# Attention's value products on four column tiles, with the row sums of later units added up on GpSimd first

## The reference

```python
q = (h @ q_w.T + q_b).reshape(b, s, 16, 32)
k = h @ k_w.T + k_b                     # (b, s, 32)
v = h @ v_w.T + v_b                     # (b, s, 32)
scores = einsum('bqhd,bkd->bhqk', q, k) / 32 ** 0.5   # causal mask
attn = softmax(scores, axis=-1)
out = einsum('bhqk,bkd->bqhd', attn, v).reshape(b, s, 512)
return out @ o_w.T + o_b
```

## Time and profile before

| | |
|---|---|
| time, median of 3 runs | 1993.2 us (1989.5, 1994.91, 1993.2) |
| profiled execution, first to last instruction (span) | 1990.9 us |
| mean granted PE clock | 0.991 |
| busy: PE, PEld | 1929.1 us, 1506.0 us |
| busy: DVE, ACT, POOL | 1379.4 us, 860.8 us, 243.7 us |
| value products (L1946), PE busy | 278.3 us |
| masks (L1083), POOL busy | 144.5 us |
| copies out (L951), ACT busy | 76.5 us |

### The profile page before, as it was taken

The page is one execution under the profiler, slowest core; times in us unless marked ns, Lnnn a source line. Parts: engine busy times, 40 slices in busy tenths (PEclk is TensorE's granted clock), DMA queues, the critical chain, the costliest instruction groups (busy, mean ns, idle before and its releaser), DMA issues.

```text
span 1990.9 us, 31329 instructions
## 1 busy us (share of the span) xinstructions
PE 1929.1 (97%) x10816; PEld 1506.0 (76%) x10816; DVE 1379.4 (69%) x3296; ACT 860.8 (43%) x1615; POOL 243.7 (12%) x589
## 2 busy tenths in 40 slices
PE   6999999999999999999999999999999999999998
PEld 3566666666666556556888889999999999999997
DVE  5687777677768656685466887777676777767755
ACT  3366565555556554474222442333333323333221
POOL 2121113211221112122010010010010100101000
PEclk8899999999999999999999999999999999999999
DMA  7443343434433565646346989779788797787884
GB/s 229 129 111 77 91 126 100 112 86 110 108 108 80 143 175 163 207 154 202 137 138 240 360 322 344 286 295 345 285 297 323 294 350 290 292 328 289 326 309 165
DMA packets 116309, 424.32 MB, mean 213 GB/s; under 512 B 28076, under 2 KB 33452, under 8 KB 101944
## 3 DMA queue, kind: packets, MB, share of 16 engines
q1 hardware_dynamic: 104488, 371.92, 55.7%
q10 hardware_dynamic: 11664, 50.40, 6.7%
HBM read 318.16 MB, written 61.10 MB: 190 GB/s over the span
## 4 chain that ended last, share of the span: by engine, by line
PE 47%; DVE 4%; ACT 2%; DMA 1%; issue 1%; SPq 0%; POOL 0%; DVEq 0%; ACTq 0%
PE banks L1786 22%; PE banks L1877 15%; PE banks L1656 8%; PE banks L1946 1%; DVE ln_stats L1220 1%; PE banks L1752 1%; PE banks L1746 1%; DMA upgate_items_dram<-items_ring 1%; DVE x_normed L1232 0%; DVE y L1345 0%; DMA upgate_raw<-in_w_ug 0%; ACT silu_gate L880 0%; PE banks L1923 0%; ACT y_split L865 0%; ACT L880 0%
## 5 line engine op out<-in xcount | busy, mean ns | idle before, releaser
L1877 PE MATMUL banks<-d_ring,y_split 128*128 128x512 f32 x1536 | 377.4, 392 | 1.9 <-DVE y_split L1365 1.9
L973 ACT ACTIVATE probs<-banks 128x512 f32<-128x512 f32 x576 | 313.0, 602 | 53.6 <-PE banks L1923 51.4
L1877 PEld LDWEIGHTS banks<-d_ring,y_split 128*128 128x128 f32 x1536 | 281.7, 188 | 56.8 <-DVE y_split L1365 2.1
L1786 PE MATMUL banks<-h_t_split,items_ring 128*128 128x256 f32 x2280 | 321.1, 283 | 1.9 <-DVE both L1322 1.9
L1786 PEld LDWEIGHTS banks<-h_t_split,items_ring 128*128 128x128 f32 x2280 | 298.8, 191 | 14.0 <-ACT h_t L791 4.0
L1946 PE MATMUL banks<-probs,v_ones 128*64 128x512 f32 (+3 forms) x1536 | 278.3, 497 | 1.0 <-POOL probs L1083 1.0
L1710 PE MATMUL banks<-k_stack,q_stacks 96*128 96x512 f32 (+3 forms) x768 | 251.5, 371 | 11.3 <-DMA q_stacks<-q_split 3.0
L1923 PE MATMUL banks<-q_stacks,k_stack 98*128 98x512 f32 (+3 forms) x768 | 250.7, 368 | 3.5 <-DMA q_stacks<-neg_max_rows 1.8
L1946 PEld LDWEIGHTS banks<-probs,v_ones 128*64 128x64 f32 x1536 | 118.3, 137 | 159.6 <-issue 132.1
L1786 PE MATMUL banks<-input_sums,items_ring 128*128 128x256 f32 x1710 | 236.2, 283 | 0.0
L1083 POOL TENSOR_SCALAR_AFFINE_SELECT probs<-probs 128x128 f32<-128x128 f32 x512 | 144.5, 306 | 666.2 <-ACT probs L973 666.0
(11 more groups left out here) (179 smaller groups left out, 2281.9 us busy)
## 6 DMA issues: line engine op xcount, KB each, us to landing
items_ring<-upgate_items_dram SPq DMA_DIRECT2D x94, 1792.0 KB, 7.3
d_ring<-down_split_dram SPq DMA_DIRECT2D x128, 512.0 KB, 8.0
q_stacks<-q_split SPq DMA_DIRECT2D x192, 128.0 KB, 2.6
o_group<-o_raw SPq DMA_DIRECT2D x128, 128.0 KB, 2.4
upgate_raw<-in_w_ug SPq DMA_DIRECT2D x32, 512.0 KB, 4.3
upgate_items_dram<-items_ring ACTq DMA_DIRECT2D x8, 1792.0 KB, 7.4
upgate_items_dram<-items_made ACTq DMA_DIRECT2D x8, 1792.0 KB, 6.9
x<-in_x SPq DMA_DIRECT2D x32, 256.0 KB, 3.2
```

Of the source, the lines that this page charges most:

```text
L973: nc.scalar.activation(pr[:, u, :], score_bank[:, at % SLOTS_SCORE, :], ACT.Exp, scale=SCALE).then_inc(exped, 1)
L1786: last = nc.tensor.matmul(item_bank(g, item), weights[:, a, item, k * P:(k + 1) * P], by_key(item_input(blk, item, m))[:, k, :], start=(k ...
L1877: last = nc.tensor.matmul(acc[:, t, :], ys[s][:, a, t * P:(t + 1) * P], dr[g % D_RING][:, m, :], start=(f == 0 and a + m == 0), stop=(f == ...
```

## The change

1. `WEIGHED` now names, for each product, one of four rows of 32 columns. Row r takes the query blocks r and r + 4, so each query block's values add up on one row; the bank holds 512 columns, query blocks r and r + 4 of the values in its first two blocks. The bank's other two blocks hold row sums, made by products with a matrix of ones, for query blocks placed by the table. One bank serves a whole head, and heads take turns. Products have at most 256 columns.
2. `sum_first` and `sum_last` are new on GpSimd: the probabilities of units 3 to 6 (queries 512 to 1023, keys 0 to 511) and of unit 7's product of keys 512 to 639 are added up, and part 1 has one product of ones with that sum for each of four query blocks. Part 1 waits for it.
3. `TRIANGLES`' two blocks of one unit are masked by one instruction.
4. One copy of 128x512 a head, five gathers instead of four; `add_halves` and the addition in `invert_sums` go.
5. `probs` gets 14 slots (units 0 to 2 twice, two for the sums); part 0 now takes units 0 to 5. The first modulation weights are loaded by eight DMAs instead of four, to other places.

```diff
+PAIRS, FIRST_UNITS = 4, 3
+SUMMED_UNITS, SUM_AFTER = (3, 4, 5, 6), 7
+PR_SLOTS = 2 * FIRST_UNITS + (NU - FIRST_UNITS) + 2
+FIRST_PART_UNITS = 6
 WEIGHED = [
-    [(0, 0, 0, 0, 512, 0), (1, 4, 1, 512, 512, 0), (0, 3, 0, 512, 512, 0), (1, 1, 1, 128, 384, 0), (1, 1, 3, 384, 128, 384),
-     (0, 2, 6, 768, 256, 256), (1, 2, 2, 256, 256, 0)],
+    [(0, 0, (0, 4)), (1, 0, (1, 5)), (2, 0, (2, 6)), (3, 0, (3, 7)),
+     (1, 1, (1, 5)), (2, 1, (2, 6)), (3, 1, (3, 7)), (0, 1, (4,)), (0, 2, (4,)),
+     (2, 2, (2, 6)), (3, 2, (3, 7)), (1, "sum", ((0, 2), (6, 6))), (0, "sum", ((0, 3), (6, 7))),
+     (1, 2, (5,)), (2, 6, (6,)), (3, 6, (7,))],
...
+def probs_slot(H, u):
+    return H % 2 * FIRST_UNITS + u if u < FIRST_UNITS else FIRST_UNITS + u
@@ SP, gather
-                for half in range(2):
-                    sp.dma_start(og[j * HD:(j + 1) * HD, 2 * half, :], oraw[2 * half * HD:(2 * half + 1) * HD, H % 2, :]).then_inc(gathered[H % 2], 16)
+                for pair in range(PAIRS):
+                    at = (PAIRS - 1 - pair) * 2 * P
+                    sp.dma_start(og[j * HD:(j + 1) * HD, G % 2, at:at + 2 * P], oraw[pair * HD:(pair + 1) * HD, H % 2, 0:2 * P]).then_inc(gathered[H % 2], 16)
@@ ACT, step
-                    if H:
-                        act.wait_ge(pv_done, (H - 1) * PARTS_OF_HEAD + (1 if u <= PART_ENDS[0] else 2))
-                    nc.scalar.activation(pr[:, u, :], score_bank[:, at % SLOTS_SCORE, :], ACT.Exp, scale=SCALE).then_inc(exped, 1)
+                    if H and u >= FIRST_UNITS:
+                        act.wait_ge(pv_done, (H - 1) * PARTS_OF_HEAD + (1 if u < FIRST_PART_UNITS else 2))
+                        act.wait_ge(summed, 3 * (H - 1) + 1)
+                    elif H >= 2:
+                        act.wait_ge(pv_done, (H - 1) * PARTS_OF_HEAD)
+                    nc.scalar.activation(pr[:, probs_slot(H, u), :], score_bank[:, at % SLOTS_SCORE, :], ACT.Exp, scale=SCALE).then_inc(exped, 1)
@@ POOL
+            def sum_first(H):
+                pool.wait_ge(exped, H * NU + SUMMED_UNITS[-1] + 1)
+                if H:
+                    pool.wait_ge(pv_done, H * PARTS_OF_HEAD)
+                first, second = (pr[:, probs_slot(H, u):probs_slot(H, u) + 2, :] for u in SUMMED_UNITS[::2])
+                nc.gpsimd.tensor_tensor(pr[:, PR_SLOTS - 2:PR_SLOTS, :], first, second, ALU.add).then_inc(summed, 1)
+                pool.wait_ge(summed, 3 * H + 1)
+                nc.gpsimd.tensor_tensor(pr[:, PR_SLOTS - 2, :], pr[:, PR_SLOTS - 2, :], pr[:, PR_SLOTS - 1, :], ALU.add).then_inc(summed, 1)
+            def sum_last(H):
+                pool.wait_ge(summed, 3 * H + 2)
+                pool.wait_ge(masked, H * len(TRIANGLES) + list(TRIANGLES).index(SUM_AFTER) + 1)
+                nc.gpsimd.tensor_tensor(pr[:, PR_SLOTS - 2, :], pr[:, PR_SLOTS - 2, :], pr[:, probs_slot(H, SUM_AFTER), :], ALU.add).then_inc(summed, 1)
...
                 for u in TRIANGLES:
+                    if u == SUM_AFTER:
+                        sum_first(H)
                     if tiles and u == BIAS_UNIT:
                         add_bias(b - 1, tiles[1])
...
+                sum_last(H)
@@ PE, weigh
                 if part == 0:
-                    pe.wait_ge(masked, H * len(TRIANGLES) + 3)
-                    pe.wait_ge(exped, H * NU + PART_ENDS[0] + 1)
+                    pe.wait_ge(masked, H * len(TRIANGLES) + FIRST_UNITS)
+                    pe.wait_ge(exped, H * NU + FIRST_PART_UNITS)
...
                 else:
                     pe.wait_ge(masked, (H + 1) * len(TRIANGLES))
+                    pe.wait_ge(summed, 3 * (H + 1))
+                for i, (row, kt, of) in enumerate(WEIGHED[part]):
+                    if kt == "sum":
+                        places, first, weights = [block(H, key, qt) for key, qt in of], 2, ones[:]
+                    else:
+                        places, first, weights = [block(H, kt, qt) for qt in of], of[0] // PAIRS, vs[:, b % 2, kt, :]
+                    moving = pr_blocks(places[0], places[-1] - places[0], len(places))
+                    out = obank[row * HD:(row + 1) * HD, H % 2, first * P:(first + len(places)) * P]
+                    last = nc.tensor.matmul(out.rearrange("p (a n) -> p a n", n=P), weights, moving, start=row not in begun, stop=part == 1 and last_of[row] == i)
```

More of the change, by code:

```diff
@@ L1162, in invert_sums @@
                 for parity in range(2):
[L1163 to L1173 removed]
+                    dve.wait_ge(gathered[parity], 160 * (G + 1))
+                nc.vector.reciprocal(sums[:], sums[:]).then_inc(sums_inverted, 1)
             def scale_group(G, half):
@@ L1441, in network @@
                     invert_sums(ALL // 4 - 1)
-                if g == 1:
-                    for half in range(2):
-                        add_halves(ALL // 4 - 1, half)
                 if nb < PLAIN and f in HAD_STEPS:
@@ L1501, in step @@
                         projection_weights(2 * PROJECTION_STEPS.index(H) + k)
-                side_step(begin[:1])
-                if begin and H > 4:
-                    for half in range(2):
-                        add_halves(G, half)
-                side_step(begin[1:])
+                side_step(begin)
                 for u in range(NU):
@@ L1870, in down @@
                             side_drained(pe, r)
-                        for c in range(2):
-                            pe.wait_ge(o_copied[c], ALL)
+                        pe.wait_ge(o_copied, ALL)
                     elif f == 0:
@@ L1925, in score, with block @@
                 last.then_inc(scored, 1)
+            def block(H, kt, qt):
+                if kt == "all":
+                    return (PR_SLOTS - 2) * HALF + (qt - PAIRS) * P
+                u, col = BLOCKS_AT[kt, qt]
+                return probs_slot(H, u) * HALF + col
             def weigh(H, part):
```

125 lines of the change are left out of this document (56 added, 69 removed), and 3 rows, old and new, of the table WEIGHED.

## The result

The changed kernel takes 2000.29 us (median of 5 runs, 1999.27 to 2001.91) beside 1993.2: ratio 1.0041, 95% interval 1.0030 to 1.0052, slower by about 7 us. 2001 was forecast. The number is right, but most of the way to it is not: two terms of more than ten microseconds each were wrong, with opposite signs. The profiled execution took 1999.27 us with a span of 1997.5.

The account below looks back on a forecast made before the run. TensorE bound the attention by averages, with VectorE level in each head's first half; TensorE's savings and delays from GpSimd's additions summed over head classes to +8.0 us: 1998.9, or 2001.2 beside the median, range 1968 to 2038.

Parts of the forecast that it names:

- -0.62 a head: TensorE's part 0 loses three blocks, 0.66 us, taken as 0.62; over 64 heads -39.7 us if nothing else ends later.
- Rival (c): Parts 0 and 1: issue of weight loads with products binds; 2077 us, half way 2035; chance 0.14 in part or whole.
- The 0.02 for tiles that lose against each other: TensorE: chance 0.02 that four tiles with short products lose against two, 0.9 us a head, 2059 us.
- GpSimd's chain: Three additions and masks each head, the third addition ending at e+6.13; e is the end of unit 6's exponential.
- The step with the most weight: VectorE instructions with two SBUF inputs, and the small negation, wait during GpSimd additions; L1135 ends at e+4.13, was e+2.66.
- rival (a): The negation slips between additions or is not wholly held, so only GpSimd's own chain counts: about 1975 us; chance 0.22.
- the 12.7 us of the plain heads: Plain heads get longer: nine with statistics by +1.13 each, +10.2 us; five without by +0.49 each, +2.5 us.
- The forecast's own sign: L1135's successor: median near 1.4 us confirms, 0.17 means rival (a); head 34's period under 9.4 or over 11.5 refutes.
- With rows: Nine heads with input rows: copy and subtraction behind the negation are held with it; +0.9 us each, +8.1 in all.
- four with 0.4 to 0.7 us more TensorE work before part 1: 0: Heads 5, 6, 13 and 29, without statistics: they add nothing to the span.
- -0.6 each: Nine heads with output tiles, nine with folds: TensorE's extra work covers the 6.2 us of sums; -10.8 us in all.
- The last three heads: Head 63's part 1 waits 6.2 us instead of 3.1, +3.1; heads 61 and 62 meet VectorE's crossing additions, +2.4 together.

Follow-up runs that it names:

- The doubled negation: The changed kernel with the 128x8 negation of the maxima done twice in a row: 2029.51 us, ratio 1.0182 to the kernel before.
- the sums left out: The changed kernel without GpSimd's three additions a head and all waits for them, output differs: 1957.3 us, ratio 0.9825 to the kernel before.
- The filled waits: The kernel with the late wait, plus nine unread products in each step behind heads 13, 29 and 45, where TensorE was idle: 1984.55 us, ratio 0.9959.
- the late wait: The changed kernel with part 1's wait for the sums moved ahead of its last four products: 1993.32 us, ratio 1.0006 to the kernel before.

## Why the prediction was right, and where it was not

**TensorE: right.** -0.62 a head was forecast, -0.65 came, all of it in part 0. Four tiles of 32 columns run side by side: 7 blocks at 0.22 us are 1.54 of the 1.65 us. Rival (c), the limit by issue, falls: part 0 has 32 loads with their products in 1.65 us, 52 ns each, part 1 40 in 1.86, 46 ns, below the 62 ns from which the rival decides. (The prediction's "42 ns a pair" for its own plan is 49, 3.52 us over 72 pairs.) The 0.02 for tiles that lose against each other falls with it.

**GpSimd's chain: size right, 0.4 us too long.** The 128x1024 addition has a median of 2.38 us (2.45 taken), the masks together 0.65 (0.81), so the third ends at e+5.7, not e+6.13.

**The step with the most weight failed in place, not in kind.** "L1135 needs its result, meets the second addition and ends at e+4.13": in the plain heads it slips in 0.02 us ahead of it. That is the mechanism of rival (a), and it took the 12.7 us of the plain heads to 0.2. The forecast's own sign says so: the median of L1187 is 0.168 us, not near 1.4; and head 34's period is 9.40, where under 9.4 was to mean that it is wrong. I had let the held negation end 0.17 us behind the first addition (e+2.68) and the second addition start right there. But a held negation ends with the addition, as the earlier trace rows has it (511.75 and 511.72) and as it is here (504.13 and 504.10), and the second addition starts only 0.08 us behind the first, for whose semaphore it waits (504.10 to 504.18). The doubled negation shows that the hold itself is real: 1.13 us instead of 0.17, 8.3 us in the plain heads and 29 in the total. The gap of 0.08 us stood in no row of before, and (a) had 0.22 where it deserved about as much as the forecast. Its time, 1975, failed as well, by the heads that come next. With rows the same: the negation slips, but the cast behind it is held for 1.51 us, +0.36 a head instead of +0.9.

**The step "four with 0.4 to 0.7 us more TensorE work before part 1: 0" was wrong by 10.8 us**, and "-0.6 each" for heads 45 and 59 by another 8. I looked at what held part 1 there and not at which VectorE instructions read SBUF while GpSimd adds: the keys' cast and subtraction; in head 5 the negation's second half (1.14 us) and the first of the gains' products (1.35 us, 0.44 before); in head 59 a layer norm row of the feed-forward part (1.83 us, 0.76 with the sums left out) and the negation (0.84). The folds of head 59, which read a PSUM bank, keep their 0.74 us. Here are the two rows of head 5:

```profile
132.33 1.14 DVE L1187 SCALAR_TENSOR_TENSOR neg_max<-max_all,neg_max 128x8 fp32r<-128x8 f32 x1 [0.22 <-DVE neg_max L1186]
...
134.23 1.35 DVE L1631 TENSOR_SCALAR x_and_residual<-gain_parts 36x512 f32<-36x512 f32 x1
```

The prediction put the hold to the negation and, in heads with rows, to the copy and subtraction behind it, and should have put it to every such instruction beside the additions. The Trainium skill (SBUF — State Buffer, Who interferes with whom) says that whoever of the two issues first gets the shared ports for its whole instruction ("Issue order, not op shape, decides who blocks"), and it counts casts, where their operands allow it, among the instructions that use the shared ports. The trace agrees: the cast begun inside an addition takes 1.57 us against 0.45, the masks behind a held cast 1.32 against 0.65, and L1187, begun 0.02 us ahead of an addition, its 0.17.

**The clock was no term at all.** In the trace of before it is 1.00 from 80 us to the attention's end, where TensorE is busy 809.5 of 834 us. In head 13 now it is 1.00 until TensorE has waited 1.12, 0.43 and 0.57 us, and then 0.50, the lower of its two levels (1.2 of 2.4 GHz); up to 15.5 us of the change are that. The filled waits show the cause, and for three heads the size.

**The last three heads**: mechanism right (waits of 2.37, 2.08 and 4.14 us for GpSimd), +5.5 taken for +9.8; the missing 4.3 can be the clock, up to 5.2 us there, which no run tested in these heads.

**SP's queue**: "SP issues five gathers instead of four; neither is late" failed in one place, head 35 (+0.8, 1.17 us of waiting for the query stacks), where four other loads share the queue. Moving those loads took the wait away; whether the fifth gather is needed for it was not tried. **The start** was +0.5 and is -1.9: with eight loads the first product came earlier in all ten traces, but by 0.6 to 1.8 us, and the rest is the spread of single traces.

So the total hit by cancellation. Too high were the plain heads (12.5), those with rows (4.8), those before a query group (3.5) and the start (2.4), together 23.2 us; too low were heads 5, 13 and 29 (10.8), output and fold heads (6.7) and the last three (4.3), together 21.8.

## What to carry to other kernels

When work moves to GpSimd, list every VectorE instruction that reads SBUF beside it, and which comes first at each; a slip of 0.02 us decided 8 us in the plain heads here and, with what one more small instruction did elsewhere, 29 in all, so give such a step an even chance and look for an order that doesn't depend on it. Put a new wait ahead of the instruction that needs it, not of its group, and leave the new work out of the steps where it meets the others: 17 heads of 64 without it, with the late wait and earlier loads, turned +0.4% into -1.4%. A wait that leaves TensorE idle for a microsecond can cost twice that, as in head 41: 1.0 us as a wait and 1.6 as a slower clock behind it.

## What the runs showed of the hardware

- Nine useless products in each of three heads made these shorter by 5.9 us in all, by keeping the granted clock at 1.00 instead of 0.77 to 0.89.
- Weight loads of 32 columns with their products pass at 46 to 52 ns a pair on four tiles, where small transposes started 62 ns apart.
- Between two GpSimd additions of which the second waits for the first one's semaphore, 0.08 us pass, in all 64 heads. A small VectorE instruction held by the first ends 0.03 us behind it, and the next small one, begun 0.02 us ahead of the second addition, takes its 0.17 us; one that comes later takes 1.13.
- VectorE holds GpSimd as well: behind a cast that an addition had held, two masks took 1.32 us instead of 0.65.
